# Weighed corners added in pairs on VectorE, with 8 accumulating transposes a tile on TensorE in place of 16

## The reference

```python
x0 = jnp.clip(jnp.floor(x), 0.0, W - 2); y0 = ...
wx = jnp.clip(x - x0, 0.0, 1.0);         wy = ...
out = v00*(1-wx_)*(1-wy_) + v01*wx_*(1-wy_) + v10*(1-wx_)*wy_ + v11*wx_*wy_
...
sampled = bilinear_sample(feature_map, sampling_points)     # [B, 1024, 8 points, 64]
keys    = jnp.einsum('bnpc,dc->bnpd', sampled, W_k)
values  = jnp.einsum('bnpc,dc->bnpd', sampled, W_v)
scores  = jnp.einsum('bnhd,bnphd->bnhp', q, k) / jnp.sqrt(dh)
attn    = softmax(scores);  out = jnp.einsum('bnhp,bnphd->bnhd', attn, v)
```

## Time and profile before

| | |
|---|---|
| median of three runs | 2933.29 us |
| profiled execution, its span (nothing of it lies outside the span) | 3729.2 us |
| busy in it: PE, PEld, DVE | 2549.7, 1648.7, 2323.3 us |
| busy in it: ACT, POOL | 1343.0, 2145.8 us |
| mean granted TensorE clock, as a share of 2.4 GHz | 0.841 |

### The profile page before, as it was taken

One profiled execution on the slowest core, in us unless ns is written; L12 is line 12 of the kernel. 1 busy time (PEld: TensorE's weight loads), 2 busy tenths in 40 slices (PEclk: granted clock), 3 DMA queues, 4 the chain that ended last, 5 costly groups with the idle time before them and its releaser, 6 DMA issues.

```text
span 3729.2 us, 33872 instructions
## 1 busy us (share of the span) xinstructions
PE 2549.7 (68%) x10680; PEld 1648.7 (44%) x10680; DVE 2323.3 (62%) x3092; ACT 1343.0 (36%) x2326; POOL 2145.8 (58%) x2052
## 2 busy tenths in 40 slices
PE   2556767676586757758676675757667675776788
PEld 2434445444454445434444443434445443444443
DVE  3655767575576757657675666757657675666661
ACT  1323333343333324323342333324333342433364
POOL 5564666566476656656566475646657566566600
PEclk6778888888798888879887897878878888888899
DMA  4232323323233232322323232222322323232300
GB/s 142 75 96 72 96 84 89 88 87 100 74 88 92 87 91 86 98 80 79 93 84 98 72 103 77 85 86 86 94 85 82 92 85 98 81 86 82 84 10 11
DMA packets 139226, 314.68 MB, mean 84 GB/s; under 512 B 68912, under 2 KB 69296, under 8 KB 134960
## 3 DMA queue, kind: packets, MB, share of 16 engines
q0 software_dynamic: 98304, 268.57, 25.0%
q1 hardware_dynamic: 40880, 45.58, 3.7%
HBM read 305.62 MB, written 8.40 MB: 84 GB/s over the span
## 4 chain that ended last, share of the span: by engine, by line
DVE 35%; another core or an unknown queue 31%; PE 16%; issue 12%; ACT 5%; DVEq 0%; DMA 0%; ACTq 0%; SPq 0%
DVE weighed L1044 8%; PE work_ps L472 5%; DVE scores L1079 4%; PE points_ps L513 3%; DVE products L1072 3%; DVE scores L1059 3%; DVE products L1056 2%; PE work_ps L494 2%; PE work_ps L573 2%; PE kv_ps L525 1%; PE work_ps L603 1%; DVE state_p L1117 1%; DVE state_q L1114 1%; DVE state_o L1104 1%
## 5 line engine op out<-in xcount | busy, mean ns | idle before, releaser
L457 POOL DMA_INDIRECT gathered<-pixels,index x2048 | 2145.6, 1048 | 1401.4 <-DVE weighed L1044 732.0
L707 ACT ACTIVATE sampled_t<-points_ps 128x512 f32<-128x512 f32 x256 | 153.3, 599 | 1456.8 <-remote 858.2
L525 PE MATMUL kv_ps<-kv_sb,sampled_t 128*128 128x256 f32 x2048 | 513.0, 405 | 206.9 <-issue 166.9
L513 PE MATMUL points_ps<-c_sb,weighed 128*128 128x128 f32 x4096 | 540.4, 289 | 139.7 <-DVE weighed L1044 126.4
L513 PEld LDWEIGHTS points_ps<-c_sb,weighed 128*128 128x128 f32 x4096 | 503.9, 151 | 253.6 <-DVE weighed L1044 162.1
L1044 DVE TENSOR_TENSOR weighed<-gathered,mix 128x1024 f32<-128x1024 f32 x512 | 600.2, 1213 | 8.2 <-remote 6.5
L525 PEld LDWEIGHTS kv_ps<-kv_sb,sampled_t 128*128 128x128 f32 x2048 | 407.0, 203 | 305.9 <-issue 199.2
L1056 DVE TENSOR_TENSOR products<-kv_ps,queries 128x1024 f32<-128x1024 f32 x128 | 156.1, 1219 | 448.2 <-remote 417.8
L472 PE MATMUL work_ps<-hn,w_sb 128*128 128x512 f32 x544 | 316.1, 705 | 159.5 <-ACT wide L772 106.6
L1072 DVE TENSOR_TENSOR products<-kv_ps,probs 128x1024 f32<-128x1024 f32 x128 | 156.2, 1220 | 368.1 <-ACT probs L712 350.3
L603 PE MATMUL work_ps<-nm,w_sb 128*128 128x512 f32 x544 | 283.0, 602 | 8.3 <-DVE xm L1207 6.0
(11 more groups left out here) (167 smaller groups left out, 3308.9 us busy)
## 6 DMA issues: line engine op xcount, KB each, us to landing
grid_px<-grid SPq DMA_DIRECT2D x32, 1024.0 KB
gathered<-pixels,index POOLq DMA_INDIRECT x2048
out<-rm SPq DMA_DIRECT2D x32, 256.0 KB
w_sb<-weights SPq DMA_DIRECT2D x1, 1984.0 KB, 8.9
moe_hidden<-consts SPq DMA_DIRECT2D x1, 512.0 KB, 9.8
attended<-cls SPq DMA_DIRECT2D x1, 512.0 KB, 11.5
c_sb<-consts SPq DMA_DIRECT2D x1, 192.0 KB, 5.1
w_sb<-weights SPq DMA_DIRECT2D x1, 192.0 KB, 5.1
```

The source lines that it names most:

```text
L457: pool.indirect_dma_start(gathered[:, n % RING, k * PATCH:(k + 1) * PATCH], None, pixels, bass.IndirectOffsetOnAxis(ap=index[:, n // TILES ...
L513: mm = pe.matmul(points_ps[:, j * P:(j + 1) * P], weighed[:, n % 2, at:at + 2 * C], ident, is_transpose=True, start=(q == 0), stop=(q == 3))
L525: mm = pe.matmul(kv_ps[:, 2 * (n % 2) + j // 2, (j % 2) * 2 * P:(j % 2 + 1) * 2 * P], sampled_t[:, n % 2, j, :], kv_sb[:, :], start=True, ...
```

## The change

After the two multiplies DVE waits for their completion and adds one half of `weighed` to the other in place: for each pair of points the corners 0 and 1 take in the corners 2 and 3 (the outer of the two steps in q, which the new code calls x). The add is one instruction of 128x1024. `weighted`, for which PE and POOL wait, is now raised by the add. PE then transposes corners 0 and 1 alone, 8 transposes a tile. The two instruction streams differ in nothing else.

```diff
@@ sample(it, n), on PE
-                    for q in range(4):
+                    for q in range(2):
                         at = (4 * j + q) * 2 * C
                         mm = pe.matmul(points_ps[:, j * P:(j + 1) * P],
                                        weighed[:, n % 2, at:at + 2 * C], ident, is_transpose=True,
-                                       start=(q == 0), stop=(q == 3))
+                                       start=(q == 0), stop=(q == 1))
@@ weigh(it, n), on DVE
                 for e in range(2):
                     ins = dve.tensor_tensor(to[:, :, :, e, :], g[:, :, e, :, :],
                                             wt[:, :, e, :].unsqueeze(3).broadcast_to([P, HEADS // 2, 4, C]), ALU.mult)
-                ins.then_inc(weighted.sem, 1)
+                    mark(ins)
+                after(vector_steps.count)
+                near = to.rearrange("p j (x y) e c -> p j x (y e c)", x=2)
+                dve.tensor_tensor(near[:, :, 0, :], near[:, :, 0, :], near[:, :, 1, :], ALU.add).then_inc(weighted.sem, 1)
```

## The result

The changed kernel takes 3031.69 us (median of four runs, 3030.47 to 3032.33), the kernel before 2933.53 in the same series: 1.0333 times as long, 95% interval 1.032 to 1.0345, or 98 us. The forecast was slower, 3094 us, with a range from 2985 to 3205. The direction was right, and the cost was three fifths of the forecast 161 us. The time lies in the range, but not in the interval of the likeliest case (3050 to 3140): it lies in that of rival 2 (2950 to 3050), for another reason than rival 2's, as the experiments show.

What follows compares the result with a forecast made beforehand. The prediction took POOL's stream of 2048 gathers as the bound. It added 161 us for gathers held by the adds, and 0 for DVE's work and the transposes, to 2933: 3094 us, range 2985 to 3205.

Steps and rivals of the forecast that it cites:

- the likeliest case: POOL's gathers set the pace and adds lengthen them: 3094 us, interval 3050 to 3140, chance 0.50.
- rival 2: POOL is not the bound and part of the unknown waits is real: 3038 or 2970 us, chance 0.20.
- What bounds the kernel: Whole kernel: timed runs go at the pace of POOL's 2048 gathers, 2997 us from the profile without waits for DVE.
- What an instruction with two SBUF inputs does to a gather: POOL beside DVE: such a DVE instruction holds a gather, which ends 0.82 us after it; DVE keeps its 1.22.
- the gather's point at 0.13: In each POOL gather, some 0.13 us after its start: a two-SBUF-input DVE instruction holds it back there to its own end.
- 256 x 0.63 = 161 us: POOL's gathers: each of 256 adds lengthens them by 0.63 us, 161 us in all, with ends at 0 and 312.
- The add's 320 us on DVE at nothing: DVE: 256 adds of 1.25 us, 20.0 per iteration, fit in the slack under POOL's pace and cost nothing.
- The transposes at nothing: PE, line 513: half of 540.4 us goes, off the path under POOL's pace; cost 0, with -55 as the end.
- The profiled span, 3700 to 3950: Profile of the changed kernel: it still carries the unknown waits, and POOL's growth hides in its 732 us.
- Rival 1: DVE and POOL take turns, so half the tiles pay the add's full 1.25 us: 3173 us, chance 0.20.
- Rival 3: POOL's gathers are not held and DVE's 20 us per iteration fit in its slack: 2933 to 2945, chance 0.05.
- rival 4: PE decides in the timed runs, so fewer transposes save time: 2798 us, chance 0.05.

Runs made afterwards that it cites:

- The second profile: The kernel before, profiled once more with no edit, since its first profile lasted 3729 us; one run, 2936.94 us.
- the PSUM version: The changed kernel with the add's second input read from the PSUM tile of corner weights instead of SBUF; 2959.34 us, 1.008 of before.

## Why the prediction was right, and where its size was off

*What bounds the kernel.* Right. The argument was that the span less POOL's wait for DVE, 2997 us, comes near the timed 2933, while the chain without its unknown waits, 2573, does not. The second profile shows POOL's stream at 2931 (2934.9 - 3.7), and six gathers a tile show the other engines at 2619, close to those 2573. The 66 us by which 2997 was too long were in the gathers (2145.6 against 2117.5), between them (642.7 against 619.9), and after the last one (14).

*What an instruction with two SBUF inputs does to a gather.* Right in the main: a held gather ends 0.82 us after the add, as forecast, and with one input in PSUM none of 208 is held. Two parts were off. The prediction let any DVE instruction hold a gather that begins before the gather's point at 0.13; the traces want it to begin at least 0.05 before the gather itself, so the most that an add can hold is 1.04 us and not 1.22. And "the DVE instruction keeps its 1.22" holds for 253 of the 256 adds: the other three met a gather that began between 0.01 before and 0.04 after them, and took 1.25, 1.29 and 1.30. The Trainium skill, page "SBUF — State Buffer", section "Who interferes with whom", has the rule on two SBUF inputs against a GpSimd instruction that reads SBUF, with which the traces agree. The same section reports that `tensor_tensor` did not stall DMAs; for these gathers that is not so, and whether it is the reading of the row numbers or the generation of the descriptors that waits, no run here tells apart.

*The term that was mis-sized.* "256 x 0.63 = 161 us". An add holds 105 / 256 = 0.41 us. The 0.63 was the mean of three gathers that had been picked because they were held, while 53 of the 256 adds hold none. The 0.60 for a random phase took 1.22 as the most that one can hold; with the measured 1.04 the same formula gives 1.04 x 1.04 / (2 x 1.25) = 0.43, an estimate of 111 us for all of them. That this comes so near the 105 is in part luck, because the phase is not random. For 67 tiles the profile names the tile's own gathers as what the first multiply waited for; their adds hold 0.08 us on average, 5 us in all. The other 189 hold 0.53, and the 16 whose multiplies come right behind line 1140 1.01. An add that follows a landing stands at a fixed distance from the stream of gathers, and here that distance is a cheap one. The prediction had this effect in its first rival and gave it the wrong sign ("which may be the dear one"). The averages are read off the trace; no run that shifts the add by a fixed time was made, so the cause of the 0.08 is argued, not shown. The adds' 105 us are not all net: the other lines with two SBUF inputs hold 15 less than before, which gives the 90 of the gathers.

*The add's 320 us on DVE at nothing.* Right at this size to within the 24 us that the PSUM version leaves, though with some 134 us of slack left and not more. DVE was busy for 2630.5 us (forecast 2635).

*The transposes at nothing.* Right: 0 was forecast with -55 as the end, and it was +6 and +17. That a saving could cost was outside the bounds. Line 513 fell from 575.0 us in the second profile of before to 321.4, not to half, with one at 308 ns against 301.

*The profiled span, 3700 to 3950.* Wrong, with no effect on the time. It took the waits of unknown cause for something that every profile of this kernel has. They were in one execution, and the span of the changed kernel's profile was 3030. The gather's mean was forecast at 1.13 us, from 1.048 and 0.08; it went from 1.034 to 1.078.

*The rivals.* Rival 1 (DVE and POOL take turns, 3173) and rival 2 (POOL is not the bound, 3038) are refuted, although rival 2's number is the nearest to the result: the second profile has POOL at 88% of the chain, and the PSUM version takes 72 of the 98 us away at the same DVE work. After the change POOL waited for DVE once, before its first gather, which speaks against rival 1. Rival 3 (gathers are not held) and rival 4 (PE decides) fall with rows of the changed kernel and with the 2941 us of 8 transposes alone.

## What to carry to other kernels

The busiest engine need not be the one that decides: subtract, from the span, what each engine waited for the others, and hold each sum against the timed run, above all where the profile is longer than it. Where GpSimd issues indirect DMAs without a pause, the price of a VectorE instruction is not its duration but whether both of its inputs lie in SBUF; with one input in PSUM 320 us of such work cost 25 here, and the next 320, with VectorE full, 225. Look also for what holds gathers already: in the second profile of before they took 183 us more than 0.945 each, 36 of it under line 973 and 46 under the scans. Halving one line's work on an engine with slack bought nothing here and cost 6 and 17 us.

## What the runs showed of the hardware

- One execution of the same program took 3729.2 us of span and another 2934.9. In the long one 86 of the 256 copies of line 707 on ACT began over 3 us after PE's last transpose before them had ended (12.0 us in the earlier trace rows); in the second none was over 0.9 us late. What held them is open.
- The held gather's end, 0.82 us after the end of the DVE instruction, was the same under instructions of 1.22 and 2.28 us, and so was its free length of 0.945. Under the three scans of an iteration (2.34 us, two SBUF inputs) a held gather ended 0.75 after the scan.
- Who came first had the way: a gather that began at least 0.05 us after the add waited for it, and one that began at most 0.04 after it did not. In three such meetings the add was lengthened, by up to 0.07 us; otherwise it took 1225 ns against 1220 with its second input in PSUM.
- ACT took 343 ns for a scaled copy of 128x64 from SBUF to SBUF; neighbours overlap, so 1024 of them kept it busy for 255.3 us, 8.0 for an image's grid pixels, where DVE took 2.28.
